# Order of the first loads, casts and matmuls in the prologue of a conditional layer and an MoE layer

## The reference

```python
masked_w = weight * mask[None, :, :]                  # (8, 256, 256)
w_bot = jnp.einsum('bg,got->bot', y, masked_w)        # y = cond_8
x = x + jnp.einsum('bnt,bot->bno', x, w_bot) + bias
...
rw = softmax(cond_8); w, sel = top_k(rw, 2); w = w / w.sum()
out = sum over the two selected experts of w * gemma_mlp(x, gate, up, down)
x = x + out + gemma_mlp(x, shared_gate, shared_up, shared_down)
```

## Time and profile before

| | |
|---|---|
| time, median of 3 runs | 410.88 us (410.84 to 411.21) |
| the profiled execution's own time | 411.14 us |
| its span, first to last instruction | 409.1 us |
| PE busy | 404.4 us (99%), 2199 matmuls |
| POOL, DVE, ACT busy | 313.3, 301.7, 254.1 us |
| first matmul of the second layer (`first_gate_up`) starts | 14.56 us |

### The profile page before, as it was taken

One profiled execution on the slowest core, in us unless ns is written; L12 is line 12 of the kernel. 1 busy time (PEld: TensorE's weight loads), 2 busy tenths in 40 slices (PEclk: granted clock), 3 DMA queues, 4 the chain that ended last, 5 costly groups with the idle time before them and its releaser, 6 DMA issues.

```text
span 409.1 us, 7375 instructions
## 1 busy us (share of the span) xinstructions
PE 404.4 (99%) x2199; PEld 351.0 (86%) x2199; DVE 301.7 (74%) x518; ACT 254.1 (62%) x483; POOL 313.3 (77%) x322
## 2 busy tenths in 40 slices
PE   8999999999999999999999999999999999999997
PEld 5788888888888888888888888888888888889886
DVE  5788876567769888765777889857687767677784
ACT  4887776666564677664646666757455556666541
POOL 1699999999729689999625969999670977999630
PEclk9999999999999999999999999999999999999999
DMA  8653332323200623323010262223200042241201
GB/s 300 211 149 91 100 121 88 103 79 104 77 2 4 199 56 109 104 101 103 28 26 1 56 198 79 77 77 108 72 26 26 2 144 62 77 136 47 53 1 51
DMA packets 18894, 35.21 MB, mean 86 GB/s; under 512 B 2098, under 2 KB 2610, under 8 KB 18866
## 3 DMA queue, kind: packets, MB, share of 16 engines
q1 hardware_dynamic: 18576, 34.61, 27.5%
q10 hardware_dynamic: 290, 0.26, 0.2%
HBM read 32.77 MB, written 2.10 MB: 85 GB/s over the span
## 4 chain that ended last, share of the span: by engine, by line
PE 97%; DVE 1%; ACT 0%; issue 0%; POOL 0%; DVEq 0%; POOLq 0%
PE o_ps L582 16%; PE g_ps L528 11%; PE u_ps L527 11%; PE u_ps L528 11%; PE u_ps L531 11%; PE g_ps L527 10%; PE g_ps L531 10%; PE p_ps L582 9%; PE l_ps L482 2%; PE p_ps L590 2%; PE p_ps L591 1%; PE u_ps L432 1%; PE o_ps L631 0%; PE p_ps L447 0%; DVE t_raw L1000 0%; DVE out_sb L1157 0%
## 5 line engine op out<-in xcount | busy, mean ns | idle before, releaser
L1268 POOL TENSOR_TENSOR eg_lo<-raw_g,eg_hi 128x512 fp32r<-128x512 f32 x64 | 91.6, 1452 | 10.4 <-ACT eg_hi L747 10.4
L780 ACT ACTIVATE gelu<-g_ps 128x512 f32<-128x512 f32 x95 | 56.9, 599 | 53.2 <-PE g_ps L531 51.8
L1076 DVE SCALAR_TENSOR_TENSOR u_ps<-gelu,route_cur,u_ps 128x512 f32<-128x512 f32 x64 | 48.1, 752 | 50.9 <-PE u_ps L531 47.7
L1112 DVE TENSOR_TENSOR h_both<-t_raw,h_both 128x1024 fp32r<-128x1024 f32 x46 | 76.4, 1661 | 0.5 <-ACT h_both L813 0.5
L1310 POOL TENSOR_TENSOR ed_lo<-s_raw,ed_hi 128x512 fp32r<-128x512 f32 x30 | 51.7, 1722 | 0.0
L800 ACT CAST h_both<-u_ps 128x256 fp32r<-128x256 f32 x46 | 17.2, 373 | 54.8 <-DVE t_raw L1091 33.4
L528 PE MATMUL g_ps<-x_hi,eg_lo 128*128 128x512 f32 (+1 forms) x128 | 50.2, 392 | 0.0
L527 PE MATMUL g_ps<-x_hi,eg_hi 128*128 128x512 f32 (+1 forms) x128 | 50.0, 391 | 0.0
L527 PE MATMUL u_ps<-x_hi,eg_hi 128*128 128x512 f32 (+1 forms) x128 | 49.8, 389 | 0.0
L528 PE MATMUL u_ps<-x_hi,eg_lo 128*128 128x512 f32 (+1 forms) x128 | 49.8, 389 | 0.0
L813 ACT CAST h_both<-t_raw 128x1024 fp32r<-128x1024 f32 x46 | 47.9, 1041 | 0.5 <-DVE t_raw L1098 0.5
(11 more groups left out here) (232 smaller groups left out, 1048.6 us busy)
## 6 DMA issues: line engine op xcount, KB each, us to landing
raw_g<-experts SPq DMA_DIRECT2D x64, 256.0 KB, 2.8
raw_d<-experts SPq DMA_DIRECT2D x32, 256.0 KB, 2.7
raw_g<-shared SPq DMA_DIRECT2D x8, 256.0 KB, 5.5
l_raw<-l_w SPq DMA_DIRECT2D x3, 512.0 KB, 5.6
x_in<-xT SPq DMA_DIRECT2D x6, 256.0 KB, 3.7
outT<-out_sb SPq DMA_DIRECT2D x6, 256.0 KB, 3.0
raw_d<-shared SPq DMA_DIRECT2D x4, 256.0 KB, 2.9
x_in<-xT SPq DMA_DIRECT2D x1, 512.0 KB, 4.3
```

Source lines behind the costliest of these rows:

```text
L780: act.activation(gelu[:, s % 2], l0_ps if at_first(b) and s == 1 else g_ps, ACT.Gelu_apprx_tanh).then_inc(gelu_done, 1)
L1076: dve.scalar_tensor_tensor(u_ps[:, s % 2], gelu[:, s % 2], route_cur[:, k:k + 1], u_ps[:, s % 2], ALU.mult, ALU.mult).then_inc(h_done, 1)
L1112: dve.tensor_tensor(h_lo[:, at], t_raw[:], h_hi[:, at].bitcast(F32), ALU.subtract).then_inc(t_lo_done, 1)
L1268: pool.tensor_tensor(eg_lo[:, j % RING], raw_g[:, j % RAW_G], eg_hi[:, j % RING].bitcast(F32), ALU.subtract).then_inc(gu_lo_done, 1)
```

## The change

- The loads come in another order. A new input, `l0_own`, packs groups 4 to 7 of half 0 with half 0's mask and the bias, in rows of 1282 floats (5128 bytes, 641 KB in all), and is loaded second, ahead of x. Half 1's mask (128 KB) goes last of the first layer's inputs, behind `load_l0_last(1)`. Weights, masks and bias now lie in one tile, `l0_rows`.
- ACT casts half 0 of x, then the mixed half 0, then half 1 of x, where it cast both halves of x first; `scale_first` follows. `split_up(0)` goes between the two pieces of half 1.
- DVE does `combine_0(0, 0)` and `(0, 1)` ahead of four small routing instructions and `route_weigh` behind half 1; `x_lo` of both halves moves behind half 0's mask, with half 0's `l_lo` between them.
- PE takes 10 `keep_warm` matmuls of 512 columns and one of 256 where it took 5 of 512, and weaves half 1's mixes between half 0's products.

```diff
--- before.py
+++ after.py
@@ -32,7 +32,7 @@
 B11, B21, B22, T1, T3, T2, T4 = 0, 1, 2, 3, 4, 5, 6
 
 
-def build(nc, xT, cond, l0_w, l0_mask, experts, shared, outT):
+def build(nc, xT, cond, l0_w, l0_own, l0_mask, experts, shared, outT):
     B, _, HH, T = xT.shape
     G = l0_w.shape[1] * QUAD
     E, PIECES, _, W2 = experts.shape
@@ -83,8 +83,9 @@
         cond_cur = sb("cond_cur", [P, G])
         route_cur = sb("route_cur", [P, TOP_K])
 
-        l0_raw = sb("l0_raw", [P, HH, G, D])
-        mask = sb("mask", [P, HH, D + 1])
+        l0_rows = sb("l0_rows", [P, HH, G * D + D + HH])
+        l0_raw = l0_rows[:, :, 0:G * D].rearrange("p h (g d) -> p h g d", d=D)
+        mask = l0_rows[:, :, G * D:G * D + D]
         l0_hi = sb("l0_hi", [P, L0C], F32R)
         l0_lo = sb("l0_lo", [P, L0C], F32R)
         x_in = sb("x_in", [P, HH, T])
@@ -209,7 +210,7 @@
             return 2 * oh + g // QUAD if oh == 0 or g < QUAD else 3 + (g - QUAD) // 2
 
         def bias_of(oh):
-            return mask[:, oh, D:D + 1]
+            return l0_rows[:, 0, G * D + D + oh:G * D + D + oh + 1]
 
         def x1_at(t, b, hh):
 
@@ -275,11 +276,14 @@
 
             def load_l0(oh, i):
                 at = slice(QUAD * i, QUAD * (i + 1))
-                sp.dma_start(l0_raw[:, oh, at], l0_w[oh, i].rearrange("p (g d) -> p g d", d=D)).then_inc(l0_in[2 * oh + i], 16)
+                sp.dma_start(l0_raw[:, oh, at], l0_w[oh, i].rearrange("p (g d) -> p g d", d=D)).then_inc(l0_in[2 * oh], 16)
 
             def load_l0_last(i):
                 at = slice(QUAD + 2 * i, QUAD + 2 * (i + 1))
                 sp.dma_start(l0_raw[:, 1, at], l0_w[1, 1, :, bass.ds(2 * i * D, 2 * D)].rearrange("p (g d) -> p g d", d=D)).then_inc(l0_in[3 + i], 16)
+
+            def load_l0_own():
+                sp.dma_start(l0_rows[:, 0, QUAD * D:G * D + D + HH], l0_own).then_inc(l0_in[1], 16)
 
             def load_x_0():
                 sp.dma_start(x_in[:], xT[0]).then_inc(x_loaded[0], 16)
@@ -410,12 +414,12 @@
 
             sp.sem_inc(stored, 1)
             load_l0(0, 0)
+            load_l0_own()
             load_x_0()
-            load_l0(0, 1)
             load_l0(1, 0)
-            sp.dma_start(mask[:], l0_mask).then_inc(mask_in, 16)
             for i in range(2):
                 load_l0_last(i)
+            sp.dma_start(mask[:, 1], l0_mask).then_inc(mask_in, 16)
             shared_weights()
             batch_0()
             with sp.Fori(1, B - 1) as b:
@@ -450,19 +454,29 @@
 
             def first_layer_0():
 
+                pass_x(0)
                 pe.wait_ge(first_hi_done, 1)
-                for th in range(HH):
-                    first_layer_part(l0_hi, 0, th, x_hi)
+                first_layer_part(l0_hi, 0, 0, x_hi)
+                mix_l0(1, 2, first=True)
+                pass_x(1)
+                first_layer_part(l0_hi, 0, 1, x_hi)
+                mix_l0(1, 3)
+                pe.wait_ge(x_lo_done, 1)
+                first_layer_part(l0_hi, 0, 0, x_lo)
+                mix_l0(1, 5)
                 mix_l0(1, 7, last=True)
-                for th in range(HH):
-                    first_layer_part(l0_hi, 0, th, x_lo)
                 pe.wait_ge(first_lo_done, 1)
                 for th in range(HH):
-                    first_layer_part(l0_lo, 0, th, x_hi, last=(th == HH - 1))
+                    first_layer_part(l0_lo, 0, th, x_hi)
+                pass_x_rest(0)
+                pe.wait_ge(x_lo_done, 2)
+                first_layer_part(l0_hi, 0, 1, x_lo, last=True)
                 for th in range(HH):
                     pe.wait_ge(first_hi_done, 2 + th)
                     for x in (x_hi, x_lo):
                         first_layer_part(l0_hi, 1, th, x)
+                    if th == 0:
+                        pass_x_rest(1)
                 for th in range(HH):
                     pe.wait_ge(first_lo_done, 2 + th)
                     first_layer_part(l0_lo, 1, th, x_hi, last=(th == HH - 1))
@@ -657,9 +671,9 @@
                         first_layer(b + 1, 1)
 
 
-            def keep_warm(count):
+            def keep_warm(count, columns=T):
                 for _ in range(count):
-                    pe.matmul(idle_ps, zeros[:, 0:P], zeros, start=True, stop=True)
+                    pe.matmul(idle_ps[:, 0:columns], zeros[:, 0:P], zeros[:, 0:columns], start=True, stop=True)
 
             def spread_cond():
                 pe.wait_ge(ones_done, 1)
@@ -668,20 +682,15 @@
 
             pe.wait_ge(zeroed, 1)
             keep_warm(WARM_UP)
+            keep_warm(1, TH)
             spread_cond()
-            keep_warm(3)
+            keep_warm(4)
             mix_l0(0, 2, first=True)
             mix_l0(0, 3)
-            pass_x(0)
-            keep_warm(1)
-            pass_x(1)
+            keep_warm(2)
             mix_l0(0, 6)
             mix_l0(0, 7, last=True)
-            for hh in range(HH):
-                pass_x_rest(hh)
-            mix_l0(1, 2, first=True)
-            for g in (3, 5):
-                mix_l0(1, g)
+            keep_warm(3)
             first_layer_0()
             first_gate_up()
             gate_up(0, 1)
@@ -913,15 +922,15 @@
             act.activation(exps[:], shifted[:], ACT.Exp).then_inc(exp_done, 1)
             for g in DIAGS[2:]:
                 scale_ident(g)
-            for hh in range(HH):
-                split_x(0, hh)
+            split_x(0, 0)
+            split_l0_0()
+            split_x(0, 1)
             scale_first()
-            split_l0_0()
             act.activation(gelu[:, 0, 0:8], shifted[:, 0], ACT.Gelu_apprx_tanh)
             split_gate(0)
-            for th in range(HH):
-                split_l0_1(th)
+            split_l0_1(0)
             split_up(0)
+            split_l0_1(1)
             first_x1_hi(0)
             split_gate(1)
             first_x1_hi(1)
@@ -966,6 +975,8 @@
                 dve.reduce_sum(exp_sum[:], exps[:], AX_X).then_inc(weighed, 1)
                 dve.wait_ge(weighed, 1)
                 dve.reciprocal(exp_rsum[:], exp_sum[:]).then_inc(weighed, 1)
+
+            def route_probs():
                 dve.wait_ge(weighed, 2)
                 dve.tensor_tensor(probs[:], exps[:], exp_rsum[:].unsqueeze(2).to_broadcast([P, B, 8]), ALU.mult).then_inc(weighed, 1)
                 dve.wait_ge(weighed, 3)
@@ -1005,9 +1016,9 @@
                 dve.tensor_tensor(half(l0_first, 0), half(l0_first, 0), mix_ps[0], ALU.add).then_inc(first_added, 1)
 
             def apply_mask_0():
-                dve.wait_ge(mask_in, 16)
+                dve.wait_ge(l0_in[1], 16)
                 dve.wait_ge(first_added, 1)
-                dve.tensor_tensor(half(l0_first, 0), half(l0_first, 0), mask[:, 0, 0:D], ALU.mult).then_inc(first_masked, 1)
+                dve.tensor_tensor(half(l0_first, 0), half(l0_first, 0), mask[:, 0], ALU.mult).then_inc(first_masked, 1)
 
             def add_mixed_1(th):
                 at = slice(D + th * P, D + (th + 1) * P)
@@ -1017,6 +1028,7 @@
 
             def apply_mask_1(th):
                 at = slice(D + th * P, D + (th + 1) * P)
+                dve.wait_ge(mask_in, 16)
                 dve.wait_ge(first_added, 2 + th)
                 dve.tensor_tensor(l0_first[:, at], l0_first[:, at], mask[:, 1, th * P:(th + 1) * P], ALU.mult).then_inc(first_masked, 1)
 
@@ -1050,7 +1062,7 @@
             def apply_mask(b):
                 dve.wait_ge(combined, G * b)
                 acc = l0_ps[:].rearrange("p (o d) -> p o d", o=HH)
-                dve.tensor_tensor(acc, acc, mask[:, :, 0:D], ALU.mult).then_inc(masked, HH)
+                dve.tensor_tensor(acc, acc, mask, ALU.mult).then_inc(masked, HH)
 
             def split_l0(b):
                 dve.wait_ge(l0_hi_done, HH * b)
@@ -1220,25 +1232,26 @@
 
             route_top()
             route_sums()
-            route_pair()
-            route_weigh()
             combine_0(0, 0)
             combine_0(0, 1)
-            for hh in range(HH):
-                first_x_lo(hh)
+            route_probs()
+            route_pair()
             combine_0(0, 4)
             combine_0(0, 5)
             add_mixed_0()
             apply_mask_0()
+            first_x_lo(0)
+            split_l0_0()
+            first_x_lo(1)
             combine_0(1, 1)
             combine_0(1, 4)
-            split_l0_0()
             combine_0(1, 6)
             for th in range(HH):
                 add_mixed_1(th)
                 apply_mask_1(th)
             for th in range(HH):
                 split_l0_1(th)
+            route_weigh()
             for oh in range(HH):
                 first_x1_lo(oh)
             route_index()
@@ -1425,12 +1438,14 @@
     B, T, D = a["x"].shape
     G = a["L0_cond_weight"].shape[0]
     HH = D // P
+    l0_w = by_halves(a["L0_cond_weight"]).reshape(-1, QUAD, P, HH, D).transpose(3, 0, 2, 1, 4).reshape(HH, -1, P, QUAD * D)
+    l0_mask = by_halves(a["L0_cond_mask"]).reshape(P, HH, D)
     arrays = {
```

(6 more changed lines are left out.)

## The result

The changed kernel takes 412.71 us (median of 22 runs, 411.84 to 415.18), the kernel before, in the 22 runs beside it, 411.53 us. The ratio is 1.0030, with a 95% interval of 1.0021 to 1.0040: slower by 0.9 to 1.6 us, clear of the 0.2% that can be told. The forecast was no change; the measured ratio is that of rival 1 (+1.25 us). The forecast's number stood on the first three runs of the kernel before (median 410.88); its 22 runs here have 411.53, so 0.65 of the 2.0 us between forecast and result is the base and not the change.

What follows compares the result with a forecast made beforehand. The prologue, a relay among PE, DVE and ACT up to the second layer's first matmul, was taken as the bound. Half 1's cast 0.35 us earlier, seventh matmul, zeros and `route_weigh` at nothing, gave 410.7 us, range 410.0 to 411.9.

Steps and rivals of the forecast that it cites:

- rival 1: PE's clock stays low until about 8.5 us, delaying half 0's last mix: +1.25 us, 412.1 to 412.4; chance 0.18.
- The rise of the clock: PE at 2.4 GHz early, so half 0's last four mixes run from 6.1 to 7.2 us.
- x's landing as the bound: On ACT, x lands at 7.70 and is cast by 8.27, with half 0 masked already at 8.15.
- the sign of being wrong: On ACT: the forecast is wrong if half 0's mask is ready well behind x's cast; no size given.
- Half 0 on DVE: Group 4's sum starts at 6.1 us, the add of PE's part at 7.2, masked at 8.15.
- Loads: On the load queue, the 641 KB piece lands at 6.06 us, x at 7.70; nothing charged for 5128-byte rows.
- ACT and half 1: DVE's first half 1 sum at 9.96 us, ACT's cast at 12.30, 0.35 earlier than before.
- The break-even point: On PE, half 0's last mix at 7.65 us decides the case; a clock rise at about 5.9 gives it.
- Zeros "cost nothing where PE waits for loads": On PE, five more matmuls on zeros and a half one were costed at nothing where PE waits for loads.
- Rival 2: Clock rise in between, or x up to 0.5 us later, passing through ACT: -0.1 to +0.5 us; chance 0.17.
- rivals 3 and 4: Half 1's last weights bound, gain 1.1 us, chance 0.08; or POOL or shared weights hold PE, gain 0 to 0.2, chance 0.10.
- the other sign of being wrong: On PE: the forecast is wrong if PE has a new wait past 15 us; no size given.

Runs made afterwards that it cites:

- e6: The kernel before with the change's extra zeros at PE's head alone, 256 columns ahead of the spread of cond and a fourth 512-column matmul behind it: 411.49 us.
- e8: The changed kernel with both of x's casts ahead of half 0's on ACT and both `x_lo` ahead of DVE's add of PE's part: 413.34 us.
- e3: The changed kernel with half 1's mixes of groups 2 and 3 ahead of PE's wait for half 0's cast: 412.51 us.
- e9: e8 with all four of half 1's mixes ahead of PE's wait for half 0's cast: 412.53 us.
- e2: The changed kernel without the two matmuls on zeros between half 0's mixes: 412.33 us.
- e7: The changed kernel with x loaded ahead of half 0's second piece, engine order unchanged: 413.50 us.
- e10: The changed kernel with the edits of e1, e2 and e9, plus ACT's casts and DVE's `x_lo` and `l_lo` reordered: 411.02 us.
- e1: The changed kernel with `route_weigh` put back ahead of DVE's sums of groups 4 and 5: 412.30 us.
- e11: The changed kernel once more, unaltered: 414.85 us in its one run.

## Why the prediction was wrong

The number failed: 410.7 forecast, with a range to 411.9, and 412.71 measured. What was forecast for rival 1, with a chance of 0.18, is what happened in the main: the low clock up to the passes of groups 6 and 7, half 0's cast at 9.66 (9.9 was named), the gate 1.37 us later (1.25 was named). That the measured 1.18 comes so near to 1.25 is partly luck: rival 1 left out the 0.7 us of `route_weigh`, and the profiles are 2.03 apart. By the forecast's own steps:

- **The rise of the clock was the step that failed.** The forecast had the last mix of half 0 done at 7.2, with PE at 2.4 GHz before 6.1. The rise came near 7.8, and the last mix was done at 8.56. The forecast took it that zeros in the gap ahead of 4.52 make an earlier rise likely, with no row to show it; e6, which adds these zeros to the kernel before, has no earlier one. In none of the ten profiles with the change's order at PE's head did the rise come early enough for 7.2; the earliest is near 6.8, in e8, with the last mix at 8.06.
- **The path was wrong with it.** The forecast had x's landing as the bound, half 0's mask being ready at 8.15 and x's first cast at 8.27. The mask was done at 9.63, 1.1 us behind that cast (8.50), and ACT waited for it. This is the sign of being wrong that the forecast named, "half 0's mask is ready well behind x's cast".
- **Half 0 on DVE**: group 4's sum at 6.1 forecast, 5.98 measured; right. The add waited for PE and came 1.5 us late (8.67 for 7.2).
- **Loads**: x at 7.70 forecast, 7.88 measured (1.78 + 6.1), the 641 KB piece at 6.06 against 5.91: right within 0.2 us. The 5128-byte rows cost nothing that shows.
- **ACT and half 1**: add to gate was 7.0 in the forecast's own steps (7.2 to 14.2) and 7.26 in the trace. The steps were read rightly, with 0.26 missing: the weave of half 1's mixes, which was to end "just ahead of DVE's need for it", made DVE wait 0.26 us (e3 removes it), and e8 and e9 show that this wait grows to 0.89 when half 0's cast is late. The seventh matmul behind the cast, costed at nothing, took 0.16.
- **What the forecast did not weigh** is that the new order takes 7.0 us from the add to the gate where the old takes 5.27. It pays only if the add is more than 1.7 us earlier. The break-even point stands in rival 1 (a last mix by 7.65), but not that the kernel's whole gain hangs on this one uncertain event.
- **`route_weigh` was costed at nothing**, "some 0.4 us, ahead of the first `x1_lo`, which waits for ACT's `x1_hi` anyway". It took 1.36 us on DVE and cost 0.7 of the total, in all six kernels that have it there. Rows that could have warned are these of the kernel before, in which a 128-column `l_lo` takes 0.28 us, and 0.61 as soon as POOL works:

```profile
13.05 0.28 DVE L1030 TENSOR_TENSOR l_lo<-t_raw,l_hi 128x128 fp32r<-128x128 f32 x1
13.50 0.61 DVE L1030 TENSOR_TENSOR l_lo<-t_raw,l_hi 128x128 fp32r<-128x128 f32 x1 [0.16 <-ACT l_hi L711]
13.22 0.74 POOL L1256 TENSOR_TENSOR sg_lo<-raw_g,sg_hi 128x256 fp32r<-128x256 f32 x1 [11.25 <-DVE t_raw L1021]
```

  The Trainium skill has a rule that bears on this: "SBUF — State Buffer", SBUF: two separate sides, says that DVE and GpSimd share one pair of ports as an exclusive lock, which a DVE instruction needs if it has two inputs in SBUF or runs in a two-port mode, and that the one that comes second waits for the other's whole instruction. The trace agrees: both instructions of `route_weigh` started behind one of POOL's and ended within 0.03 us of its end. Whether the first, which has one input, runs in such a mode, no view here shows.
- **Zeros "cost nothing where PE waits for loads"**: PE did not wait for loads at the two between the mixes. The next weights were in at 5.9 and PE ran zeros until 7.3; without them the add was 0.58 us earlier (e2). Rival 1 had named 0.9 for them. Behind the three after the mixes PE idled for 0.62 us in the change, so they cost nothing there; those at the head cost nothing that e6 could measure.
- **Rival 2, a late x as the bound**, is refuted by e7 for the change's order; **rivals 3 and 4** did not come: L526 started at 15.93, and PE had no wait ahead of L530. But PE did have a new wait past 15 us, ahead of L534, the other sign of being wrong.

Where the time went: of the 2.03 us between the two profiles, -0.62 by the earlier add, +1.68 by both `x_lo` and `l_lo` ahead of half 1, +0.15 by the mixes' wait and what goes with it, +0.16 by the seventh matmul, +0.66 by `route_weigh`. Against the forecast, which had the end 0.35 earlier and not 2.03 later, 2.38 us are to be explained: half 0's mask came 1.48 late, of which 1.26 reach DVE's first sum of half 1 (11.22 for 9.96), 0.30 were added up to the cast, 0.16 up to the gate and 0.66 behind it. So the clock and the zeros are half of the miss, and the largest part of it.

## What to carry to other kernels

A new order that starts a chain earlier but makes it longer is a bet on the event that starts it; work out the length of the chain from that event on for both orders first, and the lead that the event needs. A filler matmul costs nothing only while the next real one has nothing to work on. A small instruction on DVE was not small while POOL ran beside it: look for a place where POOL is idle, and none ahead of what PE waits for. And a gap in which one engine waits for another, as DVE's 1.62 us here, is the place for work that would otherwise stand in the chain (e10).

## What the runs showed of the hardware

- An 8-column instruction on DVE, 0.17 us alone, took 0.66 to 0.70 us beside POOL's 256-column subtractions, and ended when they did.
- The rise from 1.2 to 2.4 GHz differs between runs by about 2 us (6.5 and 8.5 in the kernel before, 6.8 and 9.0 in e8 and e3, which are alike on PE up to there), and the granted clock of the profile's windows shows 1.00 at both levels; here only the spacing of the matmuls tells.
- The same load lands at different times in different runs: the kernel before's second piece at 7.4 and at 8.2 us, its mask at 9.3 and at 10.2, with the gate at 14.56 and at 15.28.
- The last stores land 2.3 to 2.5 us behind DVE's last instruction in twelve profiles and 4.3 to 4.4 behind it in two (e1, e11); the executions are as much longer.
